# Cosine attention: node-block pairs computed once, their exponentials turned by DMA transposes

## What is computed

```python
Wh = h @ W.T
norms = jnp.linalg.norm(Wh, axis=1, keepdims=True)
sim = Wh @ Wh.T / (norms * norms.T + EPS)
mask = (adj > 0) | jnp.eye(N, dtype=bool)
alpha = jax.nn.softmax(jnp.where(mask, sim, -jnp.inf), axis=1)
return alpha @ Wh
```

## Time and profile before

| | |
|---|---|
| median of 3 runs | 2360.34 us (2359.82 to 2361.92) |
| profiled execution | 2360.47 us, span 2358.5 us |
| granted PE clock, mean over the span | 0.952 |
| `cosine_attend`: first matmul to last | about 765.5 to 1210 us |
| busy share of the span | PE 89%, DVE 84%, ACT 76%, POOL 31% |

### The profile page before, as it was taken

The page is one execution under the profiler, slowest core; times in us unless marked ns, Lnnn a source line. Parts: engine busy times, 40 slices in busy tenths (PEclk is TensorE's granted clock), DMA queues, the critical chain, the costliest instruction groups (busy, mean ns, idle before and its releaser), DMA issues. The chain is left out here.

```text
span 2358.5 us, 61100 instructions
## 1 busy us (share of the span) xinstructions
PE 2099.1 (89%) x24639; PEld 1644.9 (70%) x24639; DVE 1969.6 (84%) x4395; ACT 1786.9 (76%) x2267; POOL 730.2 (31%) x698
## 2 busy tenths in 40 slices
PE   4758999999957999999979599999999999895999
PEld 3548999999944888888865366666666666564554
DVE  5576999999985888888877699999999999994322
ACT  4547999999975877777755499999999999995100
POOL 0020000000000000000003488888888888871000
PEclk9958999999978999999989799999999999997999
DMA  9787212112102011011006411111111111101121
GB/s 319 266 347 287 92 63 90 66 61 89 60 6 65 30 44 44 23 44 44 23 14 135 139 61 66 67 67 66 66 66 67 67 66 59 41 5 50 58 95 66
DMA packets 78298, 199.46 MB, mean 85 GB/s; under 512 B 26868, under 2 KB 44436, under 8 KB 74690
## 3 DMA queue, kind: packets, MB, share of 16 engines
q1 hardware_dynamic: 74833, 188.31, 23.6%
q10 hardware_dynamic: 3184, 7.25, 0.8%
HBM read 160.16 MB, written 26.85 MB: 79 GB/s over the span
## 5 line engine op out<-in xcount | busy, mean ns | idle before, releaser
L1630 DVE CUSTOM_DVE_ANT_0 h_S<-h_ps,h_off 128x832 f32<-128x832 f32 x832 | 800.4, 1019 | 14.1 <-POOL h_off L1469 11.1
L1527 PE MATMUL h_ps<-KS,h_QS 98*128 98x416 f16 x1664 | 442.3, 348 | 79.8 <-DVE h_mx L1630 45.3
L1587 ACT ACTIVATE h_H<-h_S,h_nmx 128x2048 fp8e4<-128x2048 f32 x208 | 416.6, 2003 | 81.6 <-DVE h_nmx L1636 81.6
L834 ACT ACTIVATE b_CA<-b_el,HC 128x1152 fp8e4<-128x1152 f32 (+1 forms) x384 | 435.4, 1218 | 2.8 <-DMA b_el<-el_dram 2.8
L931 PE MATMUL b_pb<-b_x,b_B 128*128 128x132 f16 x5408 | 414.3, 221 | 3.9 <-DVE b_B L896 3.4
L931 PEld LDWEIGHTS b_pb<-b_x,b_B 128*128 128x128 fp8e4 x5408 | 340.3, 96 | 6.6 <-DVE b_B L896 6.2
L1475 POOL TENSOR_SCALAR h_gap<-h_S,h_nmx 128x1280 f32<-128x1280 f32 x208 | 277.0, 1332 | 90.9 <-DVE h_nmx L1636 81.4
L912 PE MATMUL b_pz<-b_x,adjT 128*128 128x134 f16 x2704 | 256.5, 222 | 16.0 <-DMA b_x<-xv_dram 16.0
L1480 POOL TENSOR_SCALAR h_H<-h_gap 128x1280 uint8<-128x1280 f32 x208 | 260.5, 1253 | 17.1
L1237 PE MATMUL c_pd<-c_mv,WnT 128*128 128x256 f16 x2028 | 251.0, 275 | 10.7 <-DMA c_ad<-adjT_dram 10.7
L1558 PEld LDWEIGHTS h_po<-Vhl,h_HT 128*128 128x128 fp8e4 x5408 | 214.7, 98 | 65.0 <-ACT h_HT L1594 0.7
(11 more groups left out here) (206 smaller groups left out, 3450.3 us busy)
## 6 DMA issues: line engine op xcount, KB each, us to landing
h_rows<-in_adj_dram SPq DMA_DIRECT2D x25, 1663.5 KB, 7.6
b_x<-xv_dram SPq DMA_DIRECT2D x48, 435.5 KB, 5.3
s_rows<-in_adj_dram SPq DMA_DIRECT2D x25, 832.0 KB, 6.6
s_rows<-in_adj_dram SPq DMA_DIRECT2D x25, 831.5 KB, 7.9
adjT_dram<-adjT SPq DMA_DIRECT2D x1, 10816.0 KB, 38.3
c_ad<-adjT_dram SPq DMA_DIRECT2D x13, 832.0 KB, 6.1
m_ad<-adjT_dram SPq DMA_DIRECT2D x13, 832.0 KB, 4.5
b_el<-el_dram SPq DMA_DIRECT2D x16, 576.0 KB, 3.8
```

The lines of the kernel that those rows point to most:

```text
L834: nc.scalar.activation(dst[:, 0:cols], elr[:, n % 2, 0:cols], ACT.Sigmoid, bias=HC[:, h, 1, jt:jt + 1], scale=STEP, saturate=False).then_i ...
L1527: last = nc.tensor.matmul(ps[:, ch % 2, b, 0:SB], QS[:, i % 2, h, :], KS[:, h, c0:c0 + SB], start=True, stop=True)
L1587: nc.scalar.activation(H[:, g % 2, 0:CA], S[:, g % 2, 0:CA], ACT.Exp, bias=nmx[:, g % 2:g % 2 + 1], scale=1.0, saturate=False).then_inc(s_ ...
L1630: nc.vector.tensor_tensor_reduce(out=two(S[:, g % 2, ch * SW:(ch + 1) * SW]), in0=ps[:, ch % 2, :, 0:SB], in1=two(off[:, i % 2, ch * SW:(c ...
```

## The change

Only the 91 pairs (c, jp) with jp >= c are computed by PE `dots`, ACT and DVE `sim`. `high` and `low` now split the unmasked exponential E into two float16 halves, which lie in one tile `U` (ring of 6). For the 78 pairs with jp > c ACT issues a DMA that stores U (256 KB) into a DRAM tensor `e_dram`. The 78 blocks with jp < c (`TURNED`) are the transposes of stored ones: SP issues a DMA transpose from `e_dram` into `G` (ring of 6, 256 KB each). POOL turns the adjacency of each of the 169 blocks into a float16 mask `MK` (0 or 1, ring of 6). `select` becomes one DVE product of 1024 float16 elements, both halves times the mask (read twice through a step of 0), from U or from G into `V` (ring of 8), which `sums` reads. `sums` is as before. The core of the diff:

```diff
+PAIRS = [(c, jp) for c in range(NC) for jp in range(c, NC)]
+TURNED = [(c, jp) for c in range(NC) for jp in range(c)]
...
+            def turned(c, jp):
+                u, m = TURNED_AT[(c, jp)], PAIR_AT[(jp, c)]
+                if u >= RG:
+                    c0, jp0 = TURNED[u - RG]
+                    sp.wait_ge(s_em, c0 * NC + jp0 + 1)
+                sp.wait_ge(s_st[m % RU], 16 * stored(m))
+                sp.dma_start(G[:, u % RG].rearrange("p a (j i) -> p (a j) i", j=2),
+                             e_dram[c * CW:(c + 1) * CW, jp].rearrange("r a i -> r (a i)"),
+                             transpose=True).then_inc(s_tr[u % RG], 16)
...
+            for c in range(1, NC):
+                for jp in range(min(c, RG)):
+                    turned(c, jp)
+                if c + 1 < NC:
+                    load(c + 1)
+                for jp in range(RG, c):
+                    turned(c, jp)
...
+            for n in range(BLOCKS):
...
+                if n >= RK:
+                    pool.wait_ge(s_em, n - RK + 1)
+                nc.gpsimd.tensor_scalar(MK[:, n % RK, :].rearrange("p (j t i) -> p j t i", j=2, t=CT),
+                                        ad[:, c % 2, :, 2 * jp:2 * jp + 2, :].rearrange("p t j i -> p j t i").bitcast(U8),
+                                        1.0 / FP8_ONE, 0.0, ALU.mult, ALU.add).then_inc(s_mk, 1)
...
+            def store(m):
...
+                act.wait_ge(s_lo, m + 1)
+                act.dma_start(e_dram[jp * CW:(jp + 1) * CW, c].rearrange("(j p) a i -> p j (a i)", p=P),
+                              U[:, m % RU].rearrange("p j a i -> p j (a i)")).then_inc(s_st[m % RU], 16)
...
+            def high(m):
+                dve.wait_ge(s_e, m + 1)
+                if m >= RU:
+                    dve.wait_ge(s_em, block_of(m - RU) + 1)
+                    dve.wait_ge(s_st[m % RU], 16 * stored(m - RU))
+                nc.vector.tensor_copy(U[:, m % RU, :, 0, :], E[:, m % RE, :].rearrange("p (j i) -> p j i", j=2)).then_inc(s_hi, 1)
...
             def select(n):
                 c, jp = n // NC, n % NC
-                dve.wait_ge(s_e, n + 1)
-                if n >= RM:
-                    dve.wait_ge(s_lo, n - RM + 1)
-                nc.vector.tensor_tensor(EM[:, n % RM, :].rearrange("p (j t i) -> p j t i", j=2, t=CT),
-                                        E[:, n % RE, :].rearrange("p (j t i) -> p j t i", j=2, t=CT),
-                                        ad[:, c % 2, :, 2 * jp:2 * jp + 2, :].rearrange("p t j i -> p j t i"), ALU.mult).then_inc(s_em, 1)
+                if jp >= c:
+                    m = PAIR_AT[(c, jp)]
+                    dve.wait_ge(s_lo, m + 1)
+                    src = U[:, m % RU].rearrange("p j a i -> p a j i")
+                else:
+                    u = TURNED_AT[(c, jp)]
+                    dve.wait_ge(s_tr[u % RG], 16 * (u // RG + 1))
+                    src = G[:, u % RG].rearrange("p a (j i) -> p a j i", j=2)
+                dve.wait_ge(s_mk, n + 1)
...
+                mask = MK[:, n % RK, :].rearrange("p (j i) -> p j i", j=2).unsqueeze(1).to_broadcast([P, 2, 2, CW])
+                nc.vector.tensor_tensor(V[:, n % RS].rearrange("p a (j i) -> p a j i", j=2), src, mask, ALU.mult).then_inc(s_em, 1)
...
+            for n in range(-SIM_AHEAD, BLOCKS):
+                if pair(n + SIM_AHEAD) is not None:
+                    sim(pair(n + SIM_AHEAD))
+                if n >= 0:
+                    c, jp = n // NC, n % NC
+                    select(n)
...
+                if pair(n + LOW_AHEAD) is not None:
+                    low(pair(n + LOW_AHEAD))
+                if pair(n + HIGH_AHEAD) is not None:
+                    high(pair(n + HIGH_AHEAD))
```

More of the change, by code:

```diff
@@ L1100, in _, with load @@
         def _(sp):
-            for c in range(NC):
+            def load(c):
                 q = c % 2
                 if c >= 2:
-                    sp.wait_ge(s_em, (c - 1) * NC)
+                    sp.wait_ge(s_t, done(c - 2))
+                    sp.wait_ge(s_mk, (c - 1) * NC)
                 sp.dma_start(mv[:, q].rearrange("p a k n -> p (a k) n"),
@@ L1135, in factor @@
                     return
[L1136 to L1142, removed]
+                act.wait_ge(s_ln, m + 1)
+                if m >= RC:
+                    act.wait_ge(s_t, m - RC + 1)
+                nc.scalar.activation(CF[:, m % RC, :], L[:, m % RL, :], ACT.Exp, scale=-1.0).then_inc(s_cf, 1)
@@ L1143, in weight @@
+            def weight(m):
+                if m >= NPAIRS:
                     return
[L1144 to L1147, removed]
+                act.wait_ge(s_t, m + 1)
+                if m >= RE:
+                    act.wait_ge(s_lo, m - RE + 1)
+                nc.scalar.activation(E[:, m % RE, :], T[:, m % RT, :], ACT.Exp, scale=1.0 / (NSC * NSC),
@@ L1148, in weight @@
                                      bias=shift[:, 0:1]).then_inc(s_e, 1)
[L1150 to L1153, removed]
-            weight(0)
[L1155 to L1158, removed]
+            def store(m):
+                c, jp = PAIRS[m]
+                if jp == c:
+                    return
+                act.wait_ge(s_lo, m + 1)
+                act.dma_start(e_dram[jp * CW:(jp + 1) * CW, c].rearrange("(j p) a i -> p j (a i)", p=P),
+                              U[:, m % RU].rearrange("p j a i -> p j (a i)")).then_inc(s_st[m % RU], 16)
@@ L1160, in _ @@
+            for m in range(3):
+                logarithm(m)
+                if m >= 1:
+                    factor(m - 1)
+            weight(0)
+            for m in range(NPAIRS):
+                logarithm(m + 3)
+                factor(m + 2)
+                weight(m + 1)
+                if m >= 1:
+                    store(m - 1)
         @block.vector
@@ L1167, in own_edges, with sim @@
                 ins.then_inc(s_own, 1)
[L1169 to L1174, removed]
+            def sim(m):
+                dve.wait_ge(s_cf, m + 1)
+                dve.wait_ge(s_dot, m + 1)
+                if m >= RT:
+                    dve.wait_ge(s_e, m - RT + 1)
+                nc.vector.tensor_tensor(T[:, m % RT, :], pd[:, m % RD, :], CF[:, m % RC, :], ALU.mult).then_inc(s_t, 1)
@@ new lines, in high, with low @@
+            def high(m):
[4 more added lines that the diff above has]
+                nc.vector.tensor_copy(U[:, m % RU, :, 0, :], E[:, m % RE, :].rearrange("p (j i) -> p j i", j=2)).then_inc(s_hi, 1)
+            def low(m):
+                dve.wait_ge(s_hi, m + 1)
+                nc.vector.tensor_tensor(U[:, m % RU, :, 1, :], E[:, m % RE, :].rearrange("p (j i) -> p j i", j=2), U[:, m % RU, :, 0, :],
+                                        ALU.subtract).then_inc(s_lo, 1)
@@ L1205, in _ @@
             own_edges(0)
[L1206 to L1221, removed]
+            for n in range(-SIM_AHEAD, BLOCKS):
+                if pair(n + SIM_AHEAD) is not None:
+                    sim(pair(n + SIM_AHEAD))
+                if n >= 0:
+                    c, jp = n // NC, n % NC
+                    select(n)
+                    if jp == FINISH_AT and c > 0:
+                        finish(c - 1)
+                    if jp == OWN_AT and c + 1 < NC:
+                        own_edges(c + 1)
+                if pair(n + LOW_AHEAD) is not None:
+                    low(pair(n + LOW_AHEAD))
+                if pair(n + HIGH_AHEAD) is not None:
+                    high(pair(n + HIGH_AHEAD))
             finish(NC - 1)
@@ L1258, in _ @@
             for n in range(DOTS_AHEAD):
-                dots(n)
+                dots(pair(n))
             for n in range(BLOCKS):
-                dots(n + DOTS_AHEAD)
+                dots(pair(n + DOTS_AHEAD))
                 sums(n)
```

78 lines of the change are left out of this document (45 added, 33 removed).

## The result

The changed kernel takes 2260.85 us (median of 4 runs, 2259.37 to 2264.32) against 2360.59 for the kernel before: ratio 0.9579, 95% interval 0.9562 to 0.9596. The forecast was 2272 with a range of 2256 to 2330. The profiled execution took 2261.32 us with a span of 2259.6.

The account below looks back on a forecast made before the run. PE was taken to pace `cosine_attend`: 342.0 us for PE, 5.3 for DVE's excess, 2 for later first sums and 7 of allowance make 356.3 against 444.5, saving 88.2; so 2272 us, range 2256 to about 2330.

Parts of the forecast that it names:

- PE's term: PE in `cosine_attend`: 3120 matmuls at 0.1096 us each make 342.0 us, 102.5 less than before.
- DVE's excess of 5.3 us: DVE's time per column exceeds PE's for k = 7 to 13 computed pairs, by 0.05 to 1.45 us, in all 5.3.
- The select's price: DVE's select of 1024 float16 elements occupies DVE 0.67 us, between bounds of 0.67 and 1.14.
- POOL's loss, 0.43 us per block: POOL's mask slips in between two DVE operations and costs DVE 0.43 us in each block.
- Case B: Rival: POOL's masks cost DVE their full time or more; 2300 us at 0.62 per block, 2347 at 0.9; chance 0.12.
- Transposes, T below 2.2: T, the spacing of queued DMA transposes into G, stays below 2.2 us; up to there nothing is lost.
- The lower bound, 0.85 us for a plain load: Lower bound for a transpose's spacing: a queue moves 256 KB in 0.85 us, read from six starting loads of 2432 KB.
- The table from T to time: Time lost by transpose spacing: nothing up to 2.2 us, then +16 us at 2.7, +49 at 3.5, +110 at 4.67.
- the break-even in a transpose's own time: Transposes served without overlap make the kernel slower from a spacing of 4.3 us; rival's chance 0.13.
- ACT's store: ACT's issue of a pair's store holds its queue 0.327 us, or 0.60 with more dimensions; hidden behind DVE's computed block.
- The allowances of 7 and 2 us: 7 us for one DVE operation of 0.6 us at each of 12 column changes; 2 us for later first sums.

Follow-up runs that it names:

- e2: The changed kernel with all 169 blocks computed, nothing stored or transposed: 2363.61 us, ratio 1.0008 to the kernel before.
- e3: The changed kernel with a float32 mask tile in place of float16: 2327.34 us, ratio 0.9854 to the kernel before.
- e1: The changed kernel with POOL making only the first six masks, which every block reuses: 2261.18 us, ratio 0.9572 to the kernel before.
- e5: The changed kernel with every transpose issued a second time, into four slots nobody reads: 2313.02 us, ratio 0.9799 to the kernel before.
- e4: The changed kernel with each transpose waiting on SP's queue until the one before has landed: 2326.66 us, ratio 0.985 to the kernel before.
- e9: The changed kernel with four slots in place of eight for the ring V: 2260.86 us, ratio 0.957 to the kernel before.
- e10: The changed kernel itself, unaltered, run again on one chip with two variants of the stage's start: 2260.99 us.

## Why the prediction was right, step by step

It was right in direction, mechanism and range; it forecast 88 us of gain where 99.2 were measured (2360.47 less 2261.32).

- **PE's term** (3120 matmuls, 342.0 us against 444.5, so 102.5 saved): right to 0.3 us. The stage lasts from the first matmul at 767.4 to the end of the last at 1113.0, 345.6 us; before it was 765.5 to 1213.3, 447.8 us, so it shrank by 102.2. e2 shows that nothing else gave any of it. Both lengths are some 3.5 us above the prediction's, and this drops out of the difference. That was partly luck: the window of the earlier trace rows ends at 1210 and leaves out 28 of 4056 matmuls (the table before the change also gives 1210 as the end), and I divided by all of them. The spacing of 0.1096 is still the right one, as a stretch at clock 1.00 of the kernel before shows (350 us / 3194):

```profile
850.00:1200.00 350.00, 350.00 (x3194) 312.18 (x3193) 306.69 (x584) 270.80 (x531) 0.00 (x0) 1.00 0.11 34
```

What each stage takes beyond its count lies mostly at its start, where the granted clock was 0.50 in both (764 to 770 us before, 762 to 768 after): the first 96 matmuls take 13.5 us before and 12.8 after, and 10.5 at 0.1096.

- **DVE's excess of 5.3 us**: a mis-sized term. The select's price was between bounds of 0.67 and 1.14 occupied, and I took 0.67; it is 0.60 (0.676 at the median less 0.08). With 0.60 the excess was 1 us, and PE's idle time says 0.3 at most. The Trainium skill (VectorE: DVE Perf Modes, "The perf-mode tier table") has all-16-bit products at two elements per cycle; the trace agrees (0.676 us against the 0.69 estimated from it), and e3 shows the other half of the rule, 1.205 at the least with one float32 operand.
- **POOL's loss, 0.43 us per block**: the place and the size for a computed block were right (0.42 in the timeline), but the turned selects lose only 0.18 on average, and half of them take 0.708 us or less, so next to nothing. In all 48 us instead of 73, none of it on the path (e1). That the cast is locked out too stood in the prediction as the Trainium skill's word alone (SBUF — State Buffer, "Who interferes with whom"); here it is 0.84 us with POOL beside it and 0.42 without. Case B did not occur: POOL's mask takes 0.617 at the least, as interpolated.
- **Transposes, T below 2.2**: right, 1.6 measured in e5. The Trainium skill's figure of 261 GB/s (DMA: Bandwidth & Descriptors, "Latency and other measured facts") would be 1.0 us; 256 KB in 1.6 us is 164 GB/s. The Trainium skill's 1309 ns for one 128x128 transpose (VectorE: DVE Perf Modes, "The three transpose paths"), added up over the eight parts of a block as in the prediction, would be 10.5 us; the page doesn't say that they add up, and the trace shows that they don't. The lower bound, 0.85 us for a plain load, was read too low from the earlier trace rows: PE waits only for the first three of the six loads, and the DMA engines moved 206 GB/s over the 8 us up to 765.4, so 1.65 MB and not 2432 KB; nothing in the sum used it. The table from T to time left out the loads in the queue: with them in the spacing it gives 61 for 66 (e4) and 46 for 52 (e5, where the last 35 pairs are 3.43 us apart, 1039.9 to 1156.4). So the break-even in a transpose's own time was somewhat nearer than the 4.3 us that I gave; where exactly is open.
- **ACT's store**: 0.378 us an issue, inside the bounds; ACT waited for `low`, and nobody for ACT but 1.3 us.
- **The allowances of 7 and 2 us**, the larger error: they were not needed. PE waited 0.3 us in all after its first matmul, and its first sums came 12.6 us after it (780.0), before the change 13.4 us (778.9). e9 shows that this isn't owed to a lead of more than four blocks. I have no run that shows how small the lead may get.

So the stage shrank by 102.2 us where 88.2 were forecast: 102.5 of PE's term less 14.3 for DVE's excess and the two allowances, of which almost nothing showed. Of the 102.2, 1.9 us went to a later first matmul (767.4 against 765.5), whose load landed later in this execution (in e10, the same kernel, it is at 765.4), and 1.4 to the part after the stage. That leaves 98.9, the difference of the spans (2358.5 and 2259.6).

## What to carry to other kernels

When one engine is busy all through a stage, count its instructions times their spacing. Take the spacing from a stretch in the middle, at full clock and with the instructions of that same stretch counted, and the stage's length from its first to its last instruction. The gain of leaving some out is that product as long as each of the other engines stays below it, and here three kinds of new work (48 us of exclusion, 78 stores, 78 transposes) fitted below it. The allowances for new waits at column changes were not needed here, with a lead of four blocks or of eight; but the room should be measured, as slowing transposes from 1.6 to 3.5 us each took back two thirds of the gain. Where a stage begins with several loads, give each its own semaphore: here PE, the first consumer, needs one of the three.

## What the runs showed of the hardware

- A POOL operation that reads SBUF holds up not only DVE products with two SBUF inputs but also DVE's float32-to-float16 cast: 0.42 us alone (e1), 0.84 with POOL in between.
- 256x512 float16 elements transposed by DMA from DRAM: about 1.6 us each in a queue that is full (e5), 3.4 us to landing when only one is under way (e4), in pieces of about 250 bytes.
- PE's granted clock in e4: 1.00 from 1000 to 1050 us with PE busy 43.8 of 50, and 0.80 from 1100 to 1175 with PE busy 46.9 of 75, in short groups of matmuls with waits between them. In stretches of 10 us within the latter it was at half (1.2 GHz, 0.50) from 1120 to 1130 with PE busy 8.3, after 5.2 in the 10 us before, and at full (2.4 GHz, 1.00) from 1140 to 1160 with PE busy 5.7 and 4.6.
